# The last layer's leaky relu: two of five row tiles as a relu on ACT and an addition on POOL

## The reference, cut to what matters

```python
h = (x @ W).reshape(n, heads, out_c)
al_s = jnp.einsum('nhc,hc->nh', h, a_src)
al_d = jnp.einsum('nhc,hc->nh', h, a_dst)
e = jax.nn.leaky_relu(al_s[src] + al_d[dst], 0.2)      # per edge
m = jax.ops.segment_max(e, dst, num_segments=n)
ex = jnp.exp(e - m[dst])
z = jax.ops.segment_sum(ex, dst, num_segments=n)
alpha = ex / (z[dst] + 1e-16)                          # softmax over a node's edges
out = jax.ops.segment_sum(h[src] * alpha[:, :, None], dst, num_segments=n)
```

## Time and profile before

| what | value |
|---|---|
| median of 3 runs | 1851.18 us (1849.32 to 1852.02) |
| the profiled execution: its time / its span | 1853.21 us / 1851.4 us |
| busy share of the span: PE, DVE, ACT, POOL | 83%, 46%, 32%, 29% |
| mean granted TensorE clock | 0.915 of 2.4 GHz |
| chain that ended last, by engine | PE 60%, DVE 13%, issue 10%, DMA 8%, ACT 6%, POOL 3% |
| last layer's head loop | from about 1614 us to about 1755 us |

### The profile page before, as it was taken

The page is one execution under the profiler, slowest core; times in us unless marked ns, Lnnn a source line. Parts: engine busy times, 40 slices in busy tenths (PEclk is TensorE's granted clock), DMA queues, the critical chain, the costliest instruction groups (busy, mean ns, idle before and its releaser), DMA issues.

```text
span 1851.4 us, 27134 instructions
## 1 busy us (share of the span) xinstructions
PE 1545.4 (83%) x10165; PEld 1489.6 (80%) x10165; DVE 859.4 (46%) x2157; ACT 584.9 (32%) x1170; POOL 533.9 (29%) x681
## 2 busy tenths in 40 slices
PE   3985889996778898976899999999999996456786
PEld 3665789896778898976899999999999996446786
DVE  5786776324366663243634223041321223489734
ACT  2223443322244433222231222222221121356521
POOL 3233332332233322313222332323232230322221
PEclk9987999997889999987899999999999998777898
DMA  2221111122211111223111122212122221100012
GB/s 86 71 75 38 46 40 30 42 79 62 75 57 46 36 33 41 78 70 107 39 38 39 55 62 59 57 55 60 33 79 78 75 75 63 55 17 1 1 46 92
DMA packets 88053, 101.63 MB, mean 55 GB/s; under 512 B 9482, under 2 KB 80673, under 8 KB 87926
## 3 DMA queue, kind: packets, MB, share of 16 engines
q1 hardware_dynamic: 71290, 68.86, 13.0%
q10 hardware_dynamic: 16636, 31.07, 5.1%
HBM read 88.12 MB, written 11.78 MB: 54 GB/s over the span
## 4 chain that ended last, share of the span: by engine, by line
PE 60%; DVE 13%; issue 10%; DMA 8%; ACT 6%; POOL 3%; DVEq 0%; ACTq 0%; POOLq 0%; SPq 0%
PE ps L785 35%; PE ps L962 6%; PE ps L848 5%; PE ps L944 4%; DVE prob L1832 3%; DMA xl<-x_scratch 2%; PE ps L815 2%; DMA stage<-in_W 2%; DVE junk L1785 2%; PE ps L920 2%; PE ps L983 1%; DMA xl<-in_x 1%; POOL pairs L1073 1%; PE ps L1006 1%; DVE prob L1840 1%
## 5 line engine op out<-in xcount | busy, mean ns | idle before, releaser
L1073 POOL TENSOR_TENSOR pairs<-stage,pairs 128x256 fp32r<-128x256 f32 (+3 forms) x472 | 367.8, 797 | 903.4 <-ACT pairs L1162 902.4
L785 PE MATMUL ps<-pairs,XB 128*125 128x256 f32 (+2 forms) x2880 | 425.1, 309 | 50.9 <-DVE asp L1785 26.0
L785 PEld LDWEIGHTS ps<-pairs,XB 128*125 128x125 f32 (+1 forms) x2880 | 414.5, 197 | 55.1 <-issue 46.4
L785 PE MATMUL ps<-pairs,XA 128*125 128x256 f32 (+3 forms) x2655 | 378.6, 304 | 7.1 <-DVE asp L1785 6.0
L785 PEld LDWEIGHTS ps<-pairs,XA 128*125 128x125 f32 (+2 forms) x2655 | 373.7, 190 | 9.2 <-DVE asp L1785 6.4
L1162 ACT ACTIVATE pairs<-stage 128x256 fp32r<-128x256 f32 (+3 forms) x472 | 189.4, 424 | 580.6 <-PE ps L785 441.8
L1488 DVE TENSOR_TENSOR Hl<-ps,Hl 125x768 fp32r<-125x768 f32 (+3 forms) x57 | 43.6, 818 | 273.3 <-ACT Hl L1212 273.3
L848 PE MATMUL ps<-AT,Hg 125*128 125x314 f32 (+1 forms) x1080 | 163.9, 311 | 6.6 <-ACT full L1220 6.6
L848 PEld LDWEIGHTS ps<-AT,Hg 125*128 125x128 f32 (+1 forms) x1080 | 158.7, 187 | 7.7 <-ACT full L1220 7.7
L815 PE MATMUL ps<-ident,prob 125*125 125x125 f32 x475 | 87.2, 335 | 83.7 <-ACT full L1220 33.6
L815 PEld LDWEIGHTS ps<-ident,prob 125*125 125x125 f32 x475 | 76.6, 240 | 90.9 <-issue 38.6
(11 more groups left out here) (211 smaller groups left out, 1686.3 us busy)
## 6 DMA issues: line engine op xcount, KB each, us to landing
stage<-in_W SPq DMA_DIRECT2D x192, 128.0 KB, 2.3
stage<-in_rel SPq DMA_DIRECT2D x99, 192.0 KB, 2.4
stage<-in_root SPq DMA_DIRECT2D x91, 64.0 KB, 1.8
x_scratch<-xo ACTq DMA_DIRECT2D x15, 375.0 KB
xl<-x_scratch ACTq DMA_DIRECT2D x15, 375.0 KB
stage<-in_rel SPq DMA_DIRECT2D x42, 128.0 KB, 2.1
stage<-in_root SPq DMA_DIRECT2D x12, 192.0 KB, 2.4
stage<-in_W SPq DMA_DIRECT2D x12, 192.0 KB, 2.5
```

The source lines that it names most:

```text
L785: last = mm(o, X[:rows, xi, a, P * (s0 + t):P * (s0 + t) + m], pair(n, b), start=k == 0 and i == 0 and t * pitch % BANK == 0, stop=k == le ...
L1073: nc.gpsimd.tensor_tensor(pair(n, 1), staged(n), pair(n, 0).bitcast(F32), ALU.subtract).then_inc(*up("weights_lo", "weights lo", n))
```

## The change

In layer 3, for its 8 heads, the row tiles d = 1 and d = 3 are computed in another form: max(s + 0.8 t, 0.2 s) = 0.2 s + relu(0.8 s + 0.8 t). ACT writes relu(0.8 s + 0.8 t) into `prob[:, d]` (one activation, the row's 0.8 t as the bias), and POOL adds `asb[:, 1]` to it in place. DVE skips these tiles. The step `mask_rows` of such a tile stands in the list at tick t - 2, behind `attention_T` and `spread`, where it was in tick t - 1 behind `scores`; the very first one (head 0, d = 1) stands in tick 0. ACT waits for the scores of the head and for the transposes of the tile that had the buffer before; POOL waits for ACT; DVE's custom instruction of the tile now waits for POOL. The last attention step (head 8) and layers 0 and 1 stay as they were.

```diff
--- before.py
+++ after.py
@@ -47,6 +47,7 @@
 GAT_HEADS = {0: (4, 512), 1: (4, 512), 3: (8, 96)}
 RGCN_IN = {1: 7, 2: 7, 3: 6}
 RGCN_CHUNKS = {1: ((0, 384), (384, 256), (640, 256)), 2: ((0, 384), (384, 384)), 3: ((0, 384), (384, 384))}
+SHARED = (1, 3)
 SCRATCH = 512
 
 
@@ -86,6 +87,10 @@
         yield ("softmax", l, h, t - 1)
     if lag <= t < NT + lag:
         yield ("attention_T", l, h, t - lag)
+
+
+def shared_mask(l, h, d):
+    return l == 3 and h < GAT_HEADS[3][0] and d in SHARED
 
 
 def rows_of(s):
@@ -237,7 +242,9 @@
                     yield ("score_sum", l, h + 1)
                 if d == NT - 1 and h + 1 < heads:
                     yield ("scores", l, h + 1)
-            if t + 1 < heads * NT:
+            if t == 0:
+                yield ("mask_rows", l, 0, 1)
+            if t + 1 < heads * NT and not shared_mask(l, (t + 1) // NT, (t + 1) % NT):
                 yield ("mask_rows", l, (t + 1) // NT, (t + 1) % NT)
             if h > 1 and d == 2:
                 yield ("elu_sum", l, h - 2, 0)
@@ -251,6 +258,8 @@
                 yield ("attention_T", l, (t - 3) // NT, (t - 3) % NT)
             if d == 2 and h + 1 < heads:
                 yield ("spread", l, h + 1)
+            if t + 2 < heads * NT and shared_mask(l, (t + 2) // NT, (t + 2) % NT):
+                yield ("mask_rows", l, (t + 2) // NT, (t + 2) % NT)
             if h and d == 4:
                 yield ("aggregate", l, h - 1, 0)
             if h > 1 and d == 0:
@@ -441,7 +450,7 @@
                  "leaky_rows", "masked", "exp_ready", "prob_step", "prob_ready", "x_bias", "att_hi",
                  "att_lo", "elu_step", "elu_exp", "x2_hi", "x2_lo", "dve_step", "count_step",
                  "bounds_step", "bounds", "count_rows", "edge_sums", "graph", "pool_const", "pool_step",
-                 "x_added", "embed", "embed_hi", "mean_step", "log_counts", "log_mask",
+                 "x_added", "relu_rows", "leaky_shared", "embed", "embed_hi", "mean_step", "log_counts", "log_mask",
                  "repeats", "repeat_step", "clones", "degree_rows", "stage_root", "stage_step"]
         names += [f"onehot{i}" for i in range(SLOTS)] + [f"onehot_used{i}" for i in range(SLOTS)]
         names += [f"x_first{d}" for d in range(NT)]
@@ -1114,7 +1123,13 @@
             for s in STEPS:
                 kind = s[0]
                 split_lo(split_limit(s))
-                if kind == "softmax" and s[2] < GAT_HEADS[s[1]][0]:
+                if kind == "mask_rows" and shared_mask(*s[1:]):
+                    l, h, d = s[1:]
+                    n = soft_order[s[1:]]
+                    pool.wait_ge(*at("relu rows", n))
+                    nc.gpsimd.tensor_tensor(prob[:, d, :N + 1], prob[:, d, :N + 1], asb[:, 1, :N + 1], ALU.add).then_inc(
+                        *up("leaky_shared", "leaky rows", n))
+                elif kind == "softmax" and s[2] < GAT_HEADS[s[1]][0]:
                     l, h, d = s[1:]
                     pool.wait_ge(*at("rden", soft_order[s[1:]]))
                     nc.gpsimd.tensor_scalar(prob[:, d, :N], prob[:, d, :N], rden[:, d:d + 1], 1.0, ALU.mult,
@@ -1311,6 +1326,14 @@
                         act.dma_start(b2b[:, :], I[f"b2_{l}"].partition_broadcast(P)).then_inc(
                             *up("bias2_in", "b2 in", l, by=16))
                         load_x(xr["output", l, 0])
+                elif kind == "mask_rows" and shared_mask(*s[1:]):
+                    l, h, d = s[1:]
+                    n = soft_order[s[1:]]
+                    act.wait_ge(*at("score rows", l, h))
+                    act.wait_ge(*at("target scores", l, h))
+                    act.wait_ge(*at("filled", "attention_T", *list(soft_order)[n - NT]))
+                    A(prob[:, d, :N + 1], asb[:, 0, :N + 1], ACT.Relu, bias=ad8[:, heads_order[l, h] % 2, d:d + 1],
+                      scale=1 - SLOPE).then_inc(*up("relu_rows", "relu rows", n))
                 elif kind == "softmax":
                     l, h, d = s[1:]
                     n = soft_order[s[1:]]
@@ -1823,6 +1846,8 @@
 
                     l, h, d = s[1:]
                     n = soft_order[s[1:]]
+                    if shared_mask(l, h, d):
+                        continue
                     dve.wait_ge(*at("score rows", l, h))
                     dve.wait_ge(*at("target scores", l, h))
                     if n >= NT:
```

## The result

The changed kernel takes 1857.28 us (median of 6 runs, 1853.1 to 1859.48), the kernel before on the same chip 1850.88 (6 runs): ratio 1.0031, 95% interval [1.0016, 1.0046]. It is slower, by 3.0 to 8.5 us. Its profiled execution is the quickest of the six: 1853.1, span 1851.3.

A forecast was written before the change was run, and what follows sets the result against it. DVE was taken to bound the head loop. +6.0 us (heads 2 to 7), +0.7 (head 1) and +1.4 (head 0) gave +8.1 on the 1851.18 median, so 1859.3; 8-in-10 range 1852 to 1865.

The forecast's parts named there:

- The exclusion, and the price of an addition: DVE's two-input SBUF instructions, L1858 and POOL exclude each other; an addition takes 1.58, of which 0.14 overlaps a wait.
- the walk: One head of the loop followed instruction by instruction: L1868 comes 1.00 later, +6.0 us for heads 2 to 7.
- ACT's part: 16 added activations on ACT, 0.73 and at most 0.82 each, hidden because ACT has room.
- The walk through tile 1: Tile 1's custom instruction waits for the addition, then POOL's scaling, and ends 0.37 later, at 1704.12.
- The place that the prediction left open: Who goes first at 1702.79: POOL's scaling (taken, +6.0 us for six heads) or DVE's custom instruction (+4.5).
- The start of the loop: Head 0, ticks 0 to 2: POOL's additions delay custom instructions and POOL's splits, +1.4 us.
- The step that failed: Tile 3's addition goes before tile 2's custom instruction, which ends 1.78 later; L1868 comes 1.00 later, 0.78 being saved.
- who came first goes first: Turn rule between POOL and DVE's excluded instructions in the loop; the held one ends about 0.67 later (0.34 for L1858).
- rival B: Tile 3's addition falls beside L1868 and the 1.30 stall; L1868 about 0.70 earlier per head, 1848.9 us; chance 0.10.
- B's condition: Tile 3's addition must reach its turn after 1706.4, 0.2 later than in the forecast's own walk.
- the end of the loop: Time gained or lost in the loop passes to the end, since PE's work behind it can't start earlier.
- the forecast's 8.1: Whole-kernel sum: +6.0 for heads 2 to 7, +0.7 for head 1, +1.4 for head 0.

The follow-up runs named there:

- run 6: Changed kernel with the addition of tiles 1 and 3 on DVE, ACT's relu kept: 1858.56 us, 1.0036 against the kernel before.
- run 1: The changed kernel again, no edit, with a second profile: 1856.31 us, 1.0023 against the kernel before.
- run 12: Changed kernel with only tile 3 shared, only heads 1 to 7, ACT's relu behind its ELU exponential: 1852.12 us, 0.9993 against the kernel before.
- run 4: Changed kernel with only tile 1 shared, tile 3 on DVE again: 1855.22 us, 1.0015 against the kernel before.
- run 7: Changed kernel with tiles 1 and 3 shared in heads 1 to 7 only, head 0 on DVE: 1854.25 us, 1.0008 against the kernel before.
- run 3: Changed kernel with only tile 3 shared, tile 1 on DVE again: 1854.02 us, 1.001 against the kernel before.
- run 8: Changed kernel with only tile 3 shared, and only in heads 1 to 7: 1854.42 us, 1.0013 against the kernel before.
- run 5: Changed kernel with a one-column DVE reciprocal between L1883 and the next custom instruction in layer 3: 1857.04 us, 1.0022 against the kernel before.
- run 2: Changed kernel with POOL's addition cut to 16 of 626 columns: 1842.75 us, 0.9953 against the kernel before.
- run 9: Changed kernel with layer 3's L1883 made a minimum with two SBUF inputs: 1864.72 us, 1.0064 against the kernel before.
- run 10: The changed kernel, no edit, profiled a third time: profiled execution 1852.6 us.

## Why the prediction was right in its sign, and where it was wrong

**The exclusion, and the price of an addition: right.** The 16-column addition shows by a change of its size alone that the additions cost some 13.5 us. The one at 1698.66 ends 1.41 after the custom instruction that it waits for, where the walk has 1.45. ACT's part is hidden in the five heads (run 6), but not always where L1883 first stands: there it waited 0.56 for ACT in the second profile (run 1), though not in the first and third, and no longer with the relu moved back (run 12).

**The walk through tile 1: right in size, in part by luck.** Tile 1 was forecast at +0.37 a head and measured at +0.34 (run 4). The 0.51 wait and the 1.39 custom instruction of the walk are there, but only in some heads. In run 4 and in the rest the custom instruction goes first, for which the walk had +0.13 up to the low part. It comes to +0.34 because the scaling then holds the copy `asad<-asp` for 0.5, an instruction that the walk didn't have among those that POOL excludes; it had the leaky instruction held there. The place that the prediction left open makes 0.1, not 0.25.

**The start of the loop: right.** +1.4 forecast, 23.42 to 23.59 measured against 22.14 and 22.29 (+1.1 to +1.5), and back to 22.27 when head 0 is left on DVE (run 7). DVE's row at 1615.21 shows the 1.45 of waiting for the addition of tile 1.

**The step that failed** is "The addition of tile 3 has stood behind it since 1706.18 and takes its turn until 1707.97. The custom instruction of tile 2 stands behind that". The rule under it, "who came first goes first", doesn't hold there. Behind L1858/L1883 the custom instruction goes first: in 37 of 37 cases in the profiles of the changed kernel and of runs 3, 7, 8 and 12, and in 5 of 5 with a reciprocal in between (run 5). The same is so in 6 of 6 with the 16-column addition (run 2). Then what rival B describes follows: the addition runs beside L1893 and the stall. Tile 3 is worth -0.79 a head (run 3), not +0.63, and both tiles -0.4 to -0.5, not +1.00. Over the five heads between the first and the sixth L1893, that is -2.2 where my walk has +5.0: 7.2 us too dear. I had taken the rule from a scaling and an addition behind custom instructions, and used it behind an instruction of another form. B's condition was wrong too: it asked that the addition come later than 1706.4, and it comes in time and loses the turn.

With another instruction ahead the forecast order does appear: run 9's period is 16.8, where the walk has 16.5 and this kernel's L1884 takes 0.3 longer. The rows of before held a place with that order, in layer 0, which I had not read:

```profile
193.70 0.42 DVE L1785 CUSTOM_DVE_ANT_0 junk<-full,ab 125x256 bf16<-125x256 f32 x1
193.70 1.90 POOL L1073 TENSOR_TENSOR pairs<-stage,pairs 128x256 fp32r<-128x256 f32 x2 [4.29 <-ACT pairs L1162]
...
194.04 0.95 DVE L1785 CUSTOM_DVE_ANT_0 junk<-full,ab 125x256 bf16<-125x256 f32 x1
```

POOL's addition waits for the instruction that runs at 193.70 and goes ahead of the one at 194.04, which is held. Between custom instructions of this form that is so in 356 of 361 cases in the fourteen profiles; in the other five POOL had begun only 0.07 or 0.08 before the first one's end.

What makes L1883 different is open. It reads one tensor in SBUF where L1884 of run 9 reads two, but that alone isn't it. In layer 2 of the kernel before, L1553 reads one tensor too (its input is uint16), POOL's addition begins 0.32 before its end, and the addition is next all the same; the custom instruction behind takes 1.64, where the same takes 0.81 at 919.83. So it is in 18 of 18 such cases. All engines:

```profile
919.83 0.81 DVE L1539 CUSTOM_DVE_ANT_0 picked<-cr_in,pick 125x625 bf16<-125x625 uint16 x1
...
920.56 0.48 DVE L1553 TENSOR_SCALAR mean<-cr_in 125x625 f32<-125x625 uint16 x1
920.72 2.74 POOL L1073 TENSOR_TENSOR pairs<-stage,pairs 128x384 fp32r<-128x384 f32 x2 [10.45 <-ACT pairs L1162]
920.96 1.64 DVE L1539 CUSTOM_DVE_ANT_0 picked<-cr_in,pick 125x625 bf16<-125x625 uint16 x1
```

Nor is it how early POOL begins: 0.37 before the end of L1883, 0.32 to 0.39 before that of L1553.

**What the prediction lacked: the end of the loop.** It was costed at nothing ("any time gained or lost in the loop passes to the end") and costs 0.7 to 3.5 us. There PE is the engine that sets the end: it works 13.47 of 16.90 us before. The chain of waits over 1735 to 1756 of the changed kernel says so, with two entries of POOL:

```profile
by line: PE ps L857 57.9%; PE ps L824 13.7%; POOL prob L1130 11.6%; DVE rl L1893 4.2%; DVE XB L1511 3.8%; POOL prob L1135 3.7%; PE ps L794 3.4%; ACT XB L1261 3.4%; DVE mn L1883 1.9%; issue 1.4%; DVEq L1892 0.1%
```

POOL's are the addition at 1734.00 and the scaling behind it, for whose result PE waits 0.58. The greater part is PE's own pace: 16.27 busy for work that took 13.47, 2.8 of the 3.3. The windows show where it is lost. In the first profile the clock is at its lower level for some 3 us in the middle of the 30 products; in the second (run 1) it is not, and PE does 21 products there instead of 13:

```profile
1750.50:1753.50 3.00, 3.00 (x13) 3.00 (x13) 1.52 (x2) 0.08 (x1) 0.00 (x0) 0.50 0.00 0
```

```profile
1750.50:1753.50 3.00, 3.00 (x21) 2.94 (x22) 1.52 (x2) 1.27 (x2) 0.00 (x0) 1.00 0.00 0
```

A lower granted clock over the whole stage (0.73 to 0.75), such a second fall in it, and an end of 18.9 to 20.2 go together in the first and third profiles of the changed kernel and in runs 3, 5, 6, 8 and 12; a single stretch at the lower level, 0.84 to 0.90 and 16.5 to 17.4 in the others, both profiles of the one before among them. The loop's period doesn't sort them: the second group has 13.99 (run 2) as well as 16.8 (run 9), and runs 7 and 10 do the same work in the loop at the same period and fall into different groups. What moves the clock to its lower level there isn't settled.

**The sum again.** From the forecast's 8.1 go 7.2 for the five heads, and 1.5 or nothing for heads 1 and 2 (+0.2 or +1.8 measured for +1.7); 3.4 or 0.7 come in at the end. That makes 2.8 by the first and third profile, 1.6 by the second, and it is within 0.2 what stands between the first leaky instruction and project2 (143.9, 144.0 and 142.6 against 141.1). So the nearness of 1859.3 to 1857.3 is in good part luck: two errors of opposite sign, and 1 to 4 us that no profile holds.

**What stays open.** The medians are 6.4 and 3.6 us above those of the kernel before. The profiles account for 2.4 on average. All three profiled executions of the changed kernel (1853.1, 1853.0, 1852.6) lie below its medians (1857.3, 1856.3) and both of the one before above theirs, and the moment at which the layer begins varies between 1610.6 and 1615.2 among executions though the code ahead of it is the same. In all three it begins earlier (1610.8 to 1612.4) than in the two of before (1614.1 and 1615.2). So the profiled executions of the changed kernel gained some 3 us in a part that the change doesn't touch, which is why they look no slower. It doesn't explain the remaining 1 to 4 us of the medians. They may be the clock in executions that weren't profiled, but nothing here shows it.

## What to carry to other kernels

Before work goes from DVE to POOL, list for each added POOL instruction the DVE instructions that exclude it, and read in the trace who wins the turn behind each form of DVE instruction: here the same addition cost nothing a head in one place (tile 3), 1.12 (0.34 and the 0.78 saved) in another (tile 1), and 1.4 in the first place once another instruction stood ahead of it on DVE (run 9's 1.7, less 0.3 by which that instruction itself is longer). Then look for the stretch that the relieved engine doesn't bound: five heads gained 2.2 to 3.9 us, and the end of the loop, bound by PE, took 0.7 to 3.5 back. A full-size and a 16-column addition, run side by side, give the price of the new work at once.

## What the runs showed of the hardware that was not expected

When a POOL addition waits behind one DVE instruction and another of two SBUF inputs stands behind that, who is next depends on the first one. Behind the two-input custom instructions (the pair at 193.70 and 194.04) and behind run 9's L1884 POOL is next (custom instruction 2.11), and behind L1553 with its one uint16 input too (1.64). Behind L1883 (one f32 input, 96x628, 0.60 us) the DVE instruction is next (0.78 to 0.79 in all of 37, and in 5 with a reciprocal between). No run here tells which property of L1883 does it.

POOL also holds small DVE instructions: the copy `asad<-asp` of 125x10 takes 0.68 instead of 0.16 behind a scaling that has the turn. The one-column reciprocals and the instructions that read PSUM keep their times beside an addition (0.15 at 1699.27, 0.81 at 1699.46).

The Trainium skill, "SBUF — State Buffer", section "SBUF: two separate sides", has the pair of SBUF ports that VectorE and GpSimd share as a lock for whoever starts first. The trace agrees where DVE is idle when POOL begins (1.35 for L1883 in run 1); it differs where both wait at the end of a third instruction: the addition begun at 1704.20 lets the custom instruction begun at 1704.49 go ahead.

POOL's addition of 125x626 takes 1.50 to 1.54 alone, and is shown for up to 2.5 when it waits (2.05 to 2.19 behind a two-input DVE instruction, about 2.5 behind L1883 and the next). The duration that the profile shows for either engine holds the wait: 2203 ns on average for the 16 additions are not their price.
